# Alternating a two-expert tile's up product with the running tile's down product, in four parts

## The reference

```python
x = x + attn(layernorm(x), Wq, Wk, Wv, Wb, Wg, Wo, norm_w)   # delta-rule linear attention, 4 heads
x = x + ffn(layernorm(x), router_w, w1, w2)

# ffn: top 2 of 8 experts for each of 4096 tokens, D = 256, H = 1024
for eid in range(e):
    w = sum(where(idx == eid, vals, 0), axis=-1)
    h = gelu(x_flat @ w1[eid].T)
    y = h @ w2[eid].T
    out = out + w[:, None] * y
```

## Time and profile before

| | |
|---|---|
| device time, median of 3 runs | 911.61 us (909.55 to 913.98) |
| span of the profiled execution | 920.4 us |
| time of the profiled execution beside its span | not listed |
| TensorE busy, matmuls | 857.0 us, 93% |
| VectorE busy | 625.7 us, 68% |
| ScalarE busy | 603.4 us, 66% |
| GpSimd busy | 438.6 us, 48% |

### The profile page before, as it was taken

One profiled execution on the slowest core, in us unless ns is written; L12 is line 12 of the kernel. 1 busy time (PEld: TensorE's weight loads), 2 busy tenths in 40 slices (PEclk: granted clock), 3 DMA queues, 4 the chain that ended last, 5 costly groups with the idle time before them and its releaser, 6 DMA issues.

```text
span 920.4 us, 29770 instructions
## 1 busy us (share of the span) xinstructions
PE 857.0 (93%) x9998; PEld 676.2 (73%) x9999; DVE 625.7 (68%) x1832; ACT 603.4 (66%) x1645; POOL 438.6 (48%) x430
## 2 busy tenths in 40 slices
PE   3799999899999999999998979999999999999995
PEld 2578877788877888778877657777778777777773
DVE  4578888798988989888885755544445555445542
ACT  3488888798888888888776725544446554445551
POOL 2154555667676676776647543322223332222333
PEclk8899999999999999999987989999999999999998
DMA  6022222233232332232233253322223333232223
GB/s 223 2 67 69 82 65 77 83 102 106 81 98 85 103 106 83 94 100 83 83 105 88 67 121 47 48 48 43 44 45 64 52 49 51 46 46 46 47 36 34
DMA packets 50653, 67.16 MB, mean 73 GB/s; under 512 B 6464, under 2 KB 35008, under 8 KB 50528
## 3 DMA queue, kind: packets, MB, share of 16 engines
q1 hardware_dynamic: 36640, 46.46, 17.5%
q0 software_dynamic: 13344, 17.97, 11.4%
q10 hardware_dynamic: 544, 1.05, 0.3%
HBM read 41.84 MB, written 23.61 MB: 71 GB/s over the span
## 4 chain that ended last, share of the span: by engine, by line
PE 58%; POOL 7%; ACT 6%; issue 6%; DMA 3%; DVE 3%; DVEq 0%; POOLq 0%; ACTq 0%
PE ps L1155 54%; DMA wst<-w 3%; ACT inverse_levels L789 2%; PE ps L1529 2%; POOL kscale L616 1%; POOL w_lo L665 1%; PE ps L1244 1%; POOL Ll L679 1%; POOL routed_rows L694 1%; POOL ors L616 1%; ACT k_sq L828 1%; POOL w_s L665 1%; ACT kq_wvg L844 1%; DVE inverse_levels L1796 1%; PE ps L1187 1%
## 5 line engine op out<-in xcount | busy, mean ns | idle before, releaser
L789 ACT ACTIVATE inverse_levels<-ps 128x512 f16<-128x512 f32 (+1 forms) x324 | 169.9, 540 | 164.8 <-PE ps L1529 140.9
L769 POOL DMA_INDIRECT out<-inverse_levels,yidx x71 | 119.4, 1682 | 259.3 <-DVE inverse_levels L2254 194.8
L1155 PE MATMUL ps<-inverse_levels,w_hi 128*128 128x256 f16 (+1 forms) x1376 | 197.9, 255 | 1.6 <-issue 1.3
L1155 PE MATMUL ps<-inverse_levels,w_lo 128*128 128x256 f16 (+1 forms) x688 | 168.1, 255 | 0.0
L2217 DVE SCALAR_TENSOR_TENSOR KpAT<-kq_wvg,inverse_levels 128x512 f16<-128x512 f32 (+1 forms) x144 | 98.8, 688 | 95.7 <-ACT inverse_levels L789 88.0
L1155 PE MATMUL ps<-w_s,inverse_levels 128*128 x426 | 140.5, 379 | 3.3 <-DVE inverse_levels L2254 2.0
L1155 PEld LDWEIGHTS ps<-inverse_levels,w_hi 128*128 x1376 | 122.6, 98 | 15.7 <-issue 3.2
L1052 ACT ACTIVATE kq_wvg<-ps 128x512 f32<-128x512 f32 (+1 forms) x144 | 85.0, 590 | 50.4 <-PE ps L1155 37.2
L1155 PE MATMUL ps<-w_s,KpAT 128*128 x426 | 116.1, 273 | 0.0
L789 ACT ACTIVATE inverse_levels<-kq_wvg 128x512 f16<-128x512 f32 (+1 forms) x144 | 89.8, 624 | 4.6
L1796 DVE CAST_PREDICATED inverse_levels<-mask_s,ps 128x256 f16<-128x256 int8 x192 | 82.0, 427 | 15.2 <-PE ps L1155 10.6
(11 more groups left out here) (239 smaller groups left out, 1922.2 us busy)
## 6 DMA issues: line engine op xcount, KB each, us to landing
wst<-w SPq DMA_DIRECT2D x58, 256.0 KB, 2.8
inverse_levels<-eye SPq DMA_DIRECT2D x35, 256.0 KB, 5.1
x_s<-x SPq DMA_DIRECT2D x32, 128.0 KB
out<-x_s SPq DMA_DIRECT2D x32, 128.0 KB, 1.7
x_s<-routed_rows SPq DMA_DIRECT2D x7, 260.0 KB
Lh<-routed_rows SPq DMA_DIRECT2D x7, 260.0 KB
Vp<-routed_rows SPq DMA_DIRECT2D x7, 260.0 KB
rowA<-routed_rows SPq DMA_DIRECT2D x7, 260.0 KB
```

The lines of the kernel that those rows point to most:

```text
L769: pool.indirect_dma_start(out=out, out_offset=bass.IndirectOffsetOnAxis(ap=yidx[:, q, a:a + 1], axis=0), in_=yrow[:, q % 2, a, :], in_offs ...
L789: return act.activation(dst, src, ACT.Copy, scale=scale)
L1155: return pe.matmul(dst, lhsT, rhs, start=start, stop=stop, **kw)
```

## The change

Where tile t + 1 is a two-expert tile (t = 7 to 14), `up(t + 1)` and `down(t)` are no longer done one after the other. Each is cut into four parts of two blocks, and they alternate: up blocks 0 and 1, down blocks 0 and 1, up 2 and 3, down 2 and 3, and so on. `down` gets an argument for its blocks. Its wait for `s_yrow` stays ahead of block 0 and its signal behind block 7. `parts_of` is now called once in each part.

```diff
--- before.py
+++ after.py
@@ -1569,12 +1569,12 @@
                     if m % 2 == 1:
                         last.then_inc(s_hps, 1)
 
-            def down(i, q):
+            def down(i, q, ms=range(KH)):
                 owners = [e for e, _ in parts_of(i, q)]
-                if not (isinstance(i, int) and i * 4 + q < 1):
+                if 0 in ms and not (isinstance(i, int) and i * 4 + q < 1):
 
                     pe.wait_ge(s_yrow, i * 4 + q)
-                for m in range(KH):
+                for m in ms:
                     if m % 2 == 0:
                         pe.wait_ge(s_hhi, i * 16 + (4 * q + m // 2 + 1))
                         pe.wait_ge(s_hlo, i * 16 + (4 * q + m // 2 + 1))
@@ -1587,7 +1587,8 @@
                         last = mm(p_yo[a][:, 0, :], hlo[:, q % 2, m, a * P:(a + 1) * P], w[:, 0:D], False, m == KH - 1)
                     if m == KH // 2 and isinstance(i, int):
                         load_experts(i * 4 + q + 2)
-                last.then_inc(s_yops, 1)
+                if KH - 1 in ms:
+                    last.then_inc(s_yops, 1)
 
             pe.wait_ge(s_xup[0], 6 * T // 2)
             xT_make(0, 0)
@@ -1644,6 +1645,11 @@
                 for q in range(first, 4):
                     if not (isinstance(i, int) and i * 4 + q + 2 >= TILES):
                         xT_make(*((i, q + 2) if not isinstance(i, int) else divmod(i * 4 + q + 2, 4)))
+                    if isinstance(i, int) and split(0, i * 4 + q + 1):
+                        for m in range(0, KH, 2):
+                            up(*divmod(i * 4 + q + 1, 4), range(m, m + 2))
+                            down(i, q, range(m, m + 2))
+                        continue
                     if not (isinstance(i, int) and i * 4 + q + 1 >= TILES):
                         up(*((i, q + 1) if not isinstance(i, int) else divmod(i * 4 + q + 1, 4)))
                     if isinstance(i, int) and i * 4 + q == TILES - 1:
```

## The result

The changed kernel takes 927.09 us (926.46 to 928.66, median of 4 runs). The kernel before took 910.62 us beside it (4 runs). The ratio is 1.0172, 95% interval 1.0152 to 1.0192: slower by 1.7%, or 15.7 us (the two medians alone lie 16.5 us apart). The forecast was slower by 12.6 us, at 924.

A forecast was written before the change was run, and what follows sets the result against it. TensorE, busy for 93% of the span, was taken as the bound, losing pace in short up matmuls. From 597.48, 15.1 + 5 x 13.8 + 13.15 + 7.2 gave 701.9 against 689.30: 12.6 us slower, 924 us, range 914 to 930.

The forecast's parts named there:

- What bounds it, and that alternation refills the lead: Up products: short matmuls use up the sequencer's lead of some 18 matmuls; alternation can win up to 1.2 us an iteration.
- the two costs: Two-expert iterations: VectorE's order delays rows_out, a 1.8 us stall; the sequencer's lead then gone, loads show as 0.7 us.
- The chain behind the last up part: End of up(t + 1) through hidden_lo and rows_out to down(t + 1): 4.89 us against 3.09 of work, stall 1.8.
- The array is late behind block 4: Each iteration t = 8 to 12: array stands 0.7 us for the sequencer's two loads; iteration 13.8 us.
- Tile 7's four loads: down(7): parts_of loads the table four times, not once, three after the stall; 15.1 us to the next down.
- Tile 14: Last alternated iteration, up parts half as long: 7.2 us to the end of the down product.
- rival (c): TensorE's clock halves for 3 us after each stall: 10 us on top, 935 us; chance 0.07.
- the likeliest case: Whole kernel: new stall each iteration and sequencer without lead behind it, slower by 12.6 us, 924 us; chance 0.62.
- Rival (a): Sequencer's lead outlasts the stall, loads done while the array waits: slower by 5.3 us, 917 up to 920; chance 0.17.
- Rival (b): Faster: hidden_lo doesn't hold rows_out up, iteration 11.5 us, whole kernel 904 to 907 us; chance 0.09.

The follow-up runs named there:

- second execution: The changed kernel run once more, unaltered, on another chip: 934.57 us against 920.65 for the kernel before, ratio 1.0156.
- the early loads in the kernel before: Kernel before, without alternation, with the table loads of tiles 8 to 15 moved into down(4), down(5) and down(6): 923.30 us, ratio 1.0044 to the kernel before.
- the run with the loads at the wait: Changed kernel with table loads moved ahead of the wait for the rows, tile 7's number read once: 926.08 us, ratio 1.0079 to the kernel before.
- both runs with loads spread: Changed kernel in two parts, table loads placed singly behind down blocks over two or three tiles: 906.47 and 905.05 us, ratios 0.9936 and 0.9932 to before.

## Why the prediction was right

The sum was made from the first matmul of down(7) to the end of down(14): 15.1 + 5 x 13.8 + 13.15 + 7.2 = 104.4 us forecast. TensorE in order of time, the last of these iterations, in the changed kernel:

```profile
684.88 0.39 PE L1155 MATMUL ps<-w_s,inverse_levels 128*128 x1 [2.15 <-DVE inverse_levels L2260]
...
693.76 0.60 PE L1529 MATMUL ps<-fc,Lh 128*128 128x128 f32 x4
```

and in its second execution:

```profile
698.22 0.39 PE L1155 MATMUL ps<-w_s,inverse_levels 128*128 x1 [2.15 <-DVE inverse_levels L2260]
...
705.44 0.60 PE L1529 MATMUL ps<-fc,Lh 128*128 128x128 f32 x4
```

down(7) starts at 586.41 in the first and at 599.83 in the second, so the whole took 107.3 and 105.6 us. Point by point:

- **What bounds it, and that alternation refills the lead**: right. The groups run at 0.17 us in every part up to the loads behind block 4; only the last three groups of the last part are slower (0.20 to 0.25 us, from 609.24). And the early loads in the kernel before show that the short matmuls are what uses the lead up. With the two costs out of the way the iteration is 11.05 to 11.08 us, the 11.0 of the prediction.
- **The chain behind the last up part**: right, 4.87 us (610.09 to 614.96) for 4.89. The stall is 1.48 for 1.8 us, since the profile counts 4.87 - 1.48 = 3.39 us as busy beside the chain in place of 3.09: the last down part and the transposes need 1.89 us (610.09 to 611.98) for 1.74, and the up part behind them ends by the profile's count 1.5 us after its start, though its groups start at the forecast pace of 1.35. Neither changes the iteration. The stalls that were forecast at about 1.8 us ahead of tiles 8 to 14 are 0.63 at tile 8, 1.44 to 1.48 at tiles 9 to 12, 1.70 at tile 13 and 2.15 at tile 14, where the up part beside the chain is half as long.
- **The array is late behind block 4**: right in kind, a little small. 0.97 us for 0.7. The parts ahead of it are also slower than the array's own pace, 1.47 and 1.39 us for 1.35. Together the last up part ends 9.26 us after down's start for 8.9, and the iteration takes 14.13 for 13.8. In five iterations this is 70.6 for 69.0 us, and tile 13's takes 13.47 for 13.15: +1.9 in all, the term that was mis-sized.
- **Tile 7's four loads**: right in kind, a little too large: 14.42 for 15.1 us. The gaps of the three behind the stall are 0.18, 0.34 and 0.70 us, ahead of the down matmuls at 589.40, 592.56 and 596.95; one of 0.61 us at 593.99 is of the two loads for tile 9. The last up part ends 9.7 us after the start for 10.2. The fourth load (at 596.0) stands behind that end and so beside the chain, which is why the wait ahead of tile 8 is only 0.63 us; the prediction didn't see this, and it costs nothing.
- **Tile 14**: 705.44 - 698.22 = 7.22 for 7.2 us in the second execution. In the first it is 693.76 - 684.88 = 8.88, by the fallen clock of rival (c), which the likeliest case put at nothing.
- **Rival (a), the lead outlasts the stall**: refuted. The loads stand at 606.5 beside the array, and moving them ahead of the wait gains 1.1 us an iteration, where an outlasting lead would have done them in the stall. The rule of the Trainium skill that I set beside it (Perfetto Trace Analysis, on the Tensor Engine instruction's life: the sequencer is free once it has pushed an instruction into the wait queue) is not refuted by this, since the wait here stands on a register operation; no run shows it on a matmul.
- **Rival (b), rows_out out of the way**: it didn't come about by itself, and its price, 11.5 us an iteration, holds where it is made to (11.62).
- **Rival (c), the clock falls after a stall**: once in 16 stalls of two executions, see below. Its price there was 1.66 us; the prediction gave it 1.5.

The sum of the differences in the first execution is -0.7 + 1.6 + 0.3 + 1.7 = +2.9 us: 12.6 + 2.9 = 15.5 us, the measured change of the stage. In the second it is +1.2, which makes 13.8. The ratios give 15.7 and 14.4. Whether the clock fell in the other timed runs too isn't shown. The forecast lies below both by the mis-sized term, and the error at tile 7 hides 0.7 us of that.

## What to carry to other kernels

An alternation that shortens the distance between a product and the wait for its buffer shortens also the time in which another engine's queue may be late: count what is written ahead of the releasing operation on that engine, and choose the grain so that the work in between is longer than that chain (here 4.9 us; two parts give 5.8, four only 3.1). Work of TensorE's sequencer costs nothing while it has a lead, and most of its time where it has none, as behind this wait on a register operation (a gap of 0.97 us for two loads of 0.65). So here the table loads belong singly among long matmuls, or ahead of a wait that will stay. Two costs that are cured singly at 1.1 to 1.2 us each may give less together, when the one was hiding a part of the other.

## What the runs showed of the hardware

**The clock after a stall.** Windows of the changed kernel (us, busy time of PE, PEld, DVE, ACT and POOL, PEclk, DMA share, GB/s):

```profile
625.00:639.00 14.00, 11.74 (x134) 8.93 (x132) 5.65 (x14) 5.47 (x9) 3.29 (x2) 1.00 0.23 39
681.00:684.90 3.90, 1.75 (x21) 1.42 (x20) 3.24 (x11) 1.85 (x4) 0.00 (x0) 1.00 0.00 0
684.90:687.00 2.10, 2.10 (x11) 1.19 (x12) 0.76 (x2) 0.00 (x0) 1.22 (x1) 0.68 0.22 30
687.00:689.00 2.00, 2.00 (x15) 1.44 (x13) 0.00 (x0) 0.74 (x2) 0.36 (x1) 0.50 0.87 172
689.00:691.00 2.00, 2.00 (x21) 1.46 (x20) 0.42 (x1) 0.38 (x2) 0.59 (x1) 0.99 0.03 4
```

Through 14 us with a stall of 1.5 us in each iteration the granted clock stays at 1.00, 2.4 GHz. In 681.0 to 684.9 TensorE was busy for 1.75 of 3.9 us, with one stand of 2.15 us; from 684.9 to 689 the clock is 0.68 and 0.50, that is 1.2 GHz for most of it, and the iteration is 1.66 us longer. In the second execution the same place has the same stand of 2.15 us, ahead of 698.22, and the clock doesn't fall. In the run with the loads at the wait TensorE stands for 2.31 us ahead of 683.63, and from 683 to 696 the clock is 1.00 too. So the length of the stand doesn't decide alone; what does stays open.

**A fallen clock that costs nothing.** At the very end of the changed kernel the step between the last two tiles' first output operations is 6.49 us for 4.81 before; the granted clock is 0.73 in 910 to 912 and 0.50 in 912 to 914 us here, and 1.00 in the kernel before from 896 to 914. From tile 16 to the end of the span both kernels need 211.7 us all the same: what follows the last output operations is 7.25 instead of 8.98 us. The end is set by GpSimd's last writes, which wait for the transfer of the ones before:

```profile
912.99 1.55 POOL L769 DMA_INDIRECT out<-inverse_levels,yidx  x1 [0.30 <-issue]
917.55 1.55 POOL L769 DMA_INDIRECT out<-inverse_levels,yidx  x1 [3.00 <-DMA out<-inverse_levels,yidx]
```

The two are 4.56 us apart here and 4.58 (908.54 to 913.12) in the kernel before. A longer step in one view is no cost before the end of the span has been looked at.

**Start of the expert tiles.** The distance from the first to the second tile's first output operation is 9.49 us in one execution of the changed kernel and 17.17 in the other, 15.1 in the kernel before's. Between the two executions of the changed kernel the spans differ by 11.7 us; this step and the next give 7.5 of it, the first tile's own start (520.61 and 526.55) 5.9, and the fallen clock takes back 1.7. On the chip on which the kernel before takes 911 to 912 us the step is 9.4 to 9.5 in both runs with loads spread; on those on which it takes 919 to 921 it is 16.45 to 17.23 in all eight traces. So spans of different executions can't be subtracted here. What decides the step stays open.
